# Lead-in of a two-layer kernel: image 0 convolved in whole chunks with a folded norm, stages without barriers

## The chip, the cores and the metric

The program runs on one core of one Trainium2 chip. The metric is the device time of one launch in microseconds, as the median of the runs. TensorE (PE) multiplies matrices and transposes, VectorE (DVE) and ScalarE (ACT) work element by element, GpSimd (POOL) computes powers and issues the gather, SyncE (SP) issues most DMAs. Each engine executes its instructions in order and waits on semaphores.

## What is computed

Four images of 384 channels and 56 x 56 pixels go through two layers, each with a residual. Cut to what matters here:

```python
# layer 0, on a group norm of x (32 groups)
value = dwconv3x3(x, w_v) ; query = dwconv3x3(x, w_q)
key   = dwconv3x3(x, w_k, stride=2) ; off = dwconv3x3(x, w_off1, stride=2)
o = gelu(layernorm_over_channels(off) * ln_g + ln_b)
pos = tanh(einsum(o, w_off2) + ref)            # 28 x 28 sampling points
v_sampled = bilinear_sample(value, pos)
attn = einsum('bcm,bcn->bmn', query, key) * SCALE
x = x + einsum(einsum(attn, v_sampled), w_out)
# layer 1, on a group norm of x
mid = silu(layernorm(xs) * ln_g + ln_b @ fc1_w + fc1_b) @ fc2_w + fc2_b
q, k, v = xs @ qkv_w ; q, k normed per head
o = norm(0.5 * v + q @ (k^T v) / pi) + mid
x = x + (o @ proj_w + proj_b)
```

Layer 0 is linear in the queries, so keys and sampled values are first multiplied into one small matrix per head, that is multiplied with `w_out` (W2T), and the "projection" is W2T times the queries.

## The kernel before

Channels are three chunks of 128 partitions; pixels are seven strips of 448 (8 rows), a strip four tiles of 112. Products that must be precise are made of three passes over a high and a low fp32r part (`WKVH`, `WKVL` and so on): `three_pass`. The program is written out by hand, engine by engine; the order in each engine's block is the order of execution, and every dependency is a semaphore.

A lead-in of four stages comes ahead of a loop over images. At the end of each stage every engine calls `stage_end` (line 292), which drains it and waits for all five.

- Stage 0 loads the weights into staging tiles (`stg`, `pst`, `qst`), folds layer norm's `ln_g` and a column centring into fc1, multiplies fc2 with proj into W2, splits the results into high and low parts, stores WKV to DRAM, and takes the group norm of image 0 from seven strips (`gn_coefs`, `gn_groups`). The small fc1-by-`ln_b` products stand first on TensorE (line 729), while the loads still run.
- Stage 1, `front(m, xg)` on each engine, seven times: ScalarE norms a strip into `XG`, VectorE does the value, key and offset taps (lines 1807, 448 or 112 columns) with the plain weights, TensorE the query taps as nine products with diagonal matrices (line 811) for each of three chunks, then transposes of values, keys and offsets; VectorE norms the offsets and takes their dot products. After the last strip come the sampling points.
- Stage 2: POOL gathers the value rows of 784 points from DRAM (`gather`, 14 indirect DMAs), VectorE mixes four neighbours (`sample_tile`), TensorE adds up key by value (`key_value`), then W2T.
- Stage 3, `project`: queries and residuals are loaded by strip, `project_strip` makes 27 passes, VectorE adds and takes the statistics of layer 1; meanwhile image 1 is read for its group norm and WKV is read back. Then `kv_start` norms the first strip, and the first key product of image 0 follows (line 892).

The image loop does layer 1 of image b, and beside it layer 0 of image b+1, which it already computes in another form than stage 1: the group norm is folded into the taps (`wfold`, `bfold`), image borders are filled with the group mean instead of zero so that the fold holds there, key and offset taps run over whole chunks of 784 outputs (line 2021), value and query taps over half chunks of 1568 (line 2233).

Of the kernel before, what the change touches and what calls it, by code (L numbers as in the profile page):

```python
# [12 lines left out]
P = 128  # L13
# [35 lines left out]
def constants():  # L49
# [6 lines left out]
    for k, (lo, hi) in enumerate(WIN):  # L56
# [6 lines left out]
    edge = np.ones((P, 2, STRIPS), f)  # L63
    edge[:, 0, 0] = 0
    edge[:, 1, STRIPS - 1] = 0
# [3 lines left out]
        "head0": head0, "head1": head1, "hsel": hsel, "refp": refp, "edge": edge,  # L69
# [3 lines left out]
def build(nc, d, out):  # L73
# [21 lines left out]
    with ctx:  # L95
# [13 lines left out]

        W1H, W1L = sb("W1H", [P, KC, HID], F32R), sb("W1L", [P, KC, HID], F32R)  # L110
        W2H, W2L = sb("W2H", [P, JC, C], F32R), sb("W2L", [P, JC, C], F32R)
        WQH, WQL = sb("WQH", [P, KC, C], F32R), sb("WQL", [P, KC, C], F32R)
        WPH, WPL = sb("WPH", [P, KC, C], F32R), sb("WPL", [P, KC, C], F32R)
# [3 lines left out]
        edge = sb("edge_s", [P, 2, STRIPS])  # L117
# [36 lines left out]
        WKVH, WKVL = sb("WKVH", [P, KC, 2 * C], F32R, at=at), sb("WKVL", [P, KC, 2 * C], F32R, at=at)  # L154
# [71 lines left out]
        at = [shared]  # L226
        pst = sb("pst", [P, KC, C], at=at)
        ones = sb("ones", [P, P], at=at)
        at = [shared + 14 * 1024]
        stg0, qst = sb("stg0", [P, KC * HID], at=at), sb("qst", [P, KC, 3 * C], at=at)  # L230
        assert at[0] <= wkv_at
        at = [base2]
        X0S = sb("X0S", [P, 3, KC, T], at=at)
        stg = [stg0, sb("stg1", [P, KC * HID], at=at)]


        at = [shared]
        diag = sb("diag", [P, KC, 9, P], at=at)
        XG2 = sb("XG2", [P, KC, RS + 2, W + 2], at=at)
        XR = sb("XR", [P, KC, RS + 2, W], at=at)  # L240
        XG = sb("XG", [P, KC, RS + 2, W + 2], at=at)
        VA, QA = sb("VA", [P, KC, T], at=at), sb("QA", [P, KC, T], at=at)
        VF = sb("VF", [TS, 2, C], at=at)
        KA, OA = sb("KA", [P, KC, TK], at=at), sb("OA", [P, KC, TK], at=at)
        KT, LN = sb("KT", [TK, C], at=at), sb("LN", [TK, C], at=at)
        olng, olnb = sb("olng", [TK, C], at=at), sb("olnb", [TK, C], at=at)
        woff2, prod = sb("woff2", [TK, 2, C], at=at), sb("prod", [TK, 2, C], at=at)
        obn, oag, orv = sb("obn", [TK, 6], at=at), sb("oag", [TK, 2], at=at), sb("orv", [TK, 2], at=at)
        dot = sb("dot", [TK, 2], at=at)
# [42 lines left out]
        def stage_end(eng, n):  # L292

            alone(eng)
            eng.drain().then_inc(stage_done, 1)
            eng.wait_ge(stage_done, n * 5 + 5)
            alone(eng)
# [2134 lines left out]
```

## Time and profile before

| | us |
|---|---|
| median of 3 runs (lowest, highest) | 3024.71 (3017.22, 3031.07) |
| profiled execution, its own time | 3018.12 |
| its span from first to last instruction | 3016.3 |
| TensorE busy | 2815.0 (93%) |
| VectorE busy | 2104.8 (70%) |
| ScalarE busy | 1201.0 (40%) |
| stages 0, 1, 2, 3 (length) | 99.4, 245.6, 44.0, 53.3 |

The stage ends are where the last engine leaves the barrier. Windows show each engine's busy time in a stretch and the clock granted to TensorE as a share of 2.4 GHz (0.50 is its lower level, 1.2 GHz). A group of the trace gives busy time, the mean length of one instruction and, behind the second bar, how long the engine stood idle before such instructions and for whom. TensorE's instructions overlap, so the distance from start to start is shorter than the length shown. An fp32 product is two instructions, one of fp32r a single one.

### The profile page before, as it was taken

What the parts mean: (1) busy time and instruction counts of PE and PEld (TensorE: products, weight loads), DVE (VectorE), ACT (ScalarE), POOL (GpSimd) and SP (SyncE); (2) the same over time, 40 slices, a digit from 0 to 9 for tenths busy, and PEclk for the clock granted to TensorE, in tenths of its full rate; (3) what the DMA queues carried; (4) which work ended last, traced back from release to release, by engine and by line L of the source; (5) the groups of instructions that cost most, each with busy time, mean ns of one, the idle gap of its engine ahead of it and who ended that gap; (6) DMA issues with size and microseconds to landing.
All of it is one profiled execution on the core that took longest, in us unless ns stands there. A gap on an engine that the chain in (4) does not pass through costs nothing.

```text
span 3016.3 us, 42244 instructions
## 1 busy us (share of the span) xinstructions
PE 2815.0 (93%) x14867; PEld 2535.9 (84%) x14867; DVE 2104.8 (70%) x3116; ACT 1201.0 (40%) x2089; POOL 690.4 (23%) x217
## 2 busy tenths in 40 slices
PE   5688578999999999999999999999999999999999
PEld 4344268989899889989999889989999899999998
DVE  3599768488888768488888768598788743444443
ACT  1433116634444226644433246544443244333332
POOL 0000104322222405222223215322223123311120
PEclk8888789999999999999999999999999999999999
DMA  5121583223322673222232763232333842111110
GB/s 203 49 79 64 159 305 124 90 66 108 108 95 93 204 257 118 84 91 91 92 123 84 248 208 114 70 111 92 102 101 114 269 173 84 34 50 37 44 40 28
DMA packets 187682, 347.54 MB, mean 115 GB/s; under 512 B 11040, under 2 KB 169312, under 8 KB 184912
## 3 DMA queue, kind: packets, MB, share of 16 engines
q1 hardware_dynamic: 180192, 320.72, 32.3%
q0 software_dynamic: 4480, 19.27, 2.2%
q10 hardware_dynamic: 2800, 4.82, 0.4%
q8 instruction: 124, 2.03, 0.3%
q14 instruction: 86, 0.70, 0.1%
HBM read 241.25 MB, written 103.51 MB: 114 GB/s over the span
## 4 chain that ended last, share of the span: by engine, by line
PE 68%; issue 12%; DVE 9%; DMA 6%; ACT 2%; POOL 1%; SPq 0%; DVEq 0%; ACTq 0%; POOLq 0%
PE bank L757 15%; PE bank L758 15%; PE bank L759 15%; PE bank L892 3%; PE bank L893 3%; PE bank L894 3%; PE bank L1092 3%; DVE VA L1807 3%; PE bank L914 3%; PE bank L1076 2%; DMA X<-x_scr 2%; DVE AC L2233 1%; DMA pair_scr<-VT 1%; PE bank L1043 1%; PE bank L1147 1%
## 5 line engine op out<-in xcount | busy, mean ns | idle before, releaser
L1567 ACT ACTIVATE S<-bank,b1p 128x448 f32<-128x448 f32 x336 | 212.9, 634 | 885.1 <-PE bank L759 864.7
L2233 DVE SCALAR_TENSOR_TENSOR AC<-XV,wfold,AC 128x1568 f32<-128x1568 f32 x288 | 530.4, 1847 | 3.1
L757 PE MATMUL bank<-SH,W2H 128*128 128x448 f32 x1008 | 394.9, 392 | 5.7 <-DVE SL L2202 5.6
L759 PE MATMUL bank<-SH,W2L 128*128 128x448 f32 x1008 | 379.6, 377 | 0.0
L758 PE MATMUL bank<-SL,W2H 128*128 128x448 f32 x1008 | 377.8, 375 | 0.0
L757 PE MATMUL bank<-XRH,W1H 128*128 128x448 f32 x1008 | 375.1, 372 | 0.0
L758 PE MATMUL bank<-XRL,W1H 128*128 128x448 f32 x1008 | 372.4, 369 | 0.0
L759 PE MATMUL bank<-XRH,W1L 128*128 128x448 f32 x1008 | 370.3, 367 | 0.0
L672 POOL TENSOR_TENSOR rq<-qn,nhalf 112x32 f32<-112x32 f32 x28 | 181.9, 6495 | 436.5 <-DVE qn L2172 436.5
L664 POOL TENSOR_TENSOR rk<-kn,nhalf 112x24 f32<-112x24 f32 (+1 forms) x56 | 200.8, 3598 | 294.5 <-DVE kn L1994 294.5
L2202 DVE TENSOR_TENSOR SL<-S,SH 128x448 fp32r<-128x448 f32 x336 | 208.0, 619 | 64.7 <-ACT SH L1570 64.6
L676 POOL TENSOR_TENSOR ro<-on,nhalf 112x32 f32<-112x32 f32 x28 | 179.8, 6422 | 311.3 <-DVE on L2193 311.2
L892 PE MATMUL bank<-WKVH,XH 128*112 128x384 f32 x672 | 234.4, 349 | 15.1 <-DVE XL L1961 7.4
L894 PE MATMUL bank<-WKVH,XL 128*112 128x384 f32 x672 | 227.8, 339 | 0.0
L893 PE MATMUL bank<-WKVL,XH 128*112 128x384 f32 x672 | 227.7, 339 | 0.0
L757 PEld LDWEIGHTS bank<-SH,W2H 128*128 128x128 f32 x1008 | 196.0, 194 | 21.8 <-issue 8.2
L759 PEld LDWEIGHTS bank<-SH,W2L 128*128 128x128 f32 x1008 | 195.8, 194 | 17.2
L758 PEld LDWEIGHTS bank<-SL,W2H 128*128 128x128 f32 x1008 | 196.5, 195 | 15.3 <-issue 0.3
L757 PEld LDWEIGHTS bank<-XRH,W1H 128*128 128x128 f32 x1008 | 193.0, 192 | 17.3
L759 PEld LDWEIGHTS bank<-XRH,W1L 128*128 128x128 f32 x1008 | 191.8, 190 | 16.7
L758 PEld LDWEIGHTS bank<-XRL,W1H 128*128 128x128 f32 x1008 | 192.0, 190 | 16.0
L1570 ACT ACTIVATE SH<-S 128x448 fp32r<-128x448 f32 x336 | 194.9, 580 | 16.3 <-ACT S L1567 0.8
(227 smaller groups left out, 5515.1 us busy)
## 6 DMA issues: line engine op xcount, KB each, us to landing
X<-x_scr SPq DMA_DIRECT2D x52, 672.0 KB, 5.3
XV<-in_xp SPq DMA_DIRECT2D x36, 870.0 KB, 6.6
CQ<-q_scr SPq DMA_DIRECT2D x28, 672.0 KB
CX<-in_x SPq DMA_DIRECT2D x28, 672.0 KB, 5.1
x_scr<-CX SPq DMA_DIRECT2D x28, 672.0 KB, 5.2
V<-v_scr SPq DMA_DIRECT2D x28, 672.0 KB, 4.7
Y<-x_scr SPq DMA_DIRECT2D x28, 672.0 KB
out<-Y SPq DMA_DIRECT2D x28, 672.0 KB, 3.8
```

The costliest lines, as they stand in the source:

```text
L664: pool.tensor_tensor(rk[:, lo:hi], kn[:, lo:hi], nhalf[0:TS, lo:hi], ALU.pow).then_inc(s["k_rs"], 1)
L672: pool.tensor_tensor(rq[:, :], qn[:, :], nhalf[0:TS, :], ALU.pow).then_inc(s["rq_s"], 1)
L757: mm(o, wh, xh, start=first, stop=False)
L758: mm(o, wh, xl, start=False, stop=False)
L759: return mm(o, wl, xh, start=False, stop=stop)
L892: mm(p, xh, WKVH[:, k, c0:c0 + C], start=(k == 0), stop=False)
L893: mm(p, xh, WKVL[:, k, c0:c0 + C], start=False, stop=False)
L894: last = mm(p, xl, WKVH[:, k, c0:c0 + C], start=False, stop=(k == KC - 1))
L1567: fn(S[:, j % 2, :], bank[j % 2][:, 0:T], ACT.Silu, bias=b1p[:, j:j + 1]).then_inc(s["s_s"], 1)
L1570: fn(SH[:, j % 3, :], S[:, j % 2, :], ACT.Copy).then_inc(s["sh"], 1)
L2202: tt(SL[:, j % 3, :], S[:, j % 2, :], f(SH[:, j % 3, :]), ALU.subtract).then_inc(s["sl"], 1)
L2233: stt(o, XV[h][:, ky:ky + HR, kx:kx + W], wfold[:, kind, k, 3 * ky + kx:3 * ky + kx + 1], o, ALU.mult, ALU.add).then_inc(s["va"], 1)
```

## The change

Image 0 is treated in the form that the image loop uses, and no stage has a barrier.

- The inputs come as three padded chunks (`XP`, 1.7 MB each) and the statistics are taken from them (`chunk_stats`); group norm is folded. Tables of the offset norm, the edge mask and `XR`, `XG` go.
- Weights are loaded into the place of their low parts (`fc1w` over `W1L`, `projw` over `WPL`, and so on) and split in place. TensorE begins with W2 (two banks instead of three), then group norm, then the fc1 and proj vector products. The splits of W1, WQ and WP and the centring of fc1 go between later work.
- Convolutions: key and offset taps on VectorE over whole chunks (`small_conv`, 48 taps); value taps of chunks 0 and 1 and query taps of chunk 2 on VectorE as six half chunks (`unit_conv`, 48 taps); value taps of chunk 2 and query taps of chunks 0 and 1 on TensorE (`front_taps`, 21 groups of nine products, with all other front work of TensorE and ScalarE placed between thirds of a group by `front_beside`).
- Offset norm, gelu and dot products are those of the image loop, on TensorE and ScalarE.
- The gather has four separate buffers; sample tiles 0 to 3 stand ahead of the last unit of query taps, 4 to 6 behind it. ScalarE issues the stores of TensorE's queries.

The diff, cut to its core:

```diff
-        def stage_end(eng, n):
-            alone(eng)
-            eng.drain().then_inc(stage_done, 1)
-            eng.wait_ge(stage_done, n * 5 + 5)
...
+            sp.dma_start(projw[:, :, :].rearrange("p k c -> p (k c)"), d["proj_w"]).then_inc(s["stg_ld1"], 16)
+            sp.dma_start(fc2w[:, :, :].rearrange("p k c -> p (k c)"), d["fc2_wT"]).then_inc(s["stg_ld1"], 16)
+            for k in range(KC):
+                sp.dma_start(XP[k][:, :, :], xpad_v[0, :, k, :, :]).then_inc(s[f"x0_ld{k}"], 16)
+            sp.dma_start(grp[:, :, :], d["grp"]).then_inc(s["grp_ld"], 16)
+            qkv_v = d["qkv_w"].rearrange("p (k c) -> p k c", k=KC)
+            sp.dma_start(kvw[:, :, :], qkv_v[:, :, C:3 * C]).then_inc(s["kvq_ld"], 16)
+            sp.dma_start(fc1w[:, :, :].rearrange("p k c -> p (k c)"), d["fc1_w"]).then_inc(s["stg_ld0"], 16)
...
+            sp.wait_ge(s["kt_st"], HEAD + 2 * KC * 16)
+            sp.wait_ge(s["gtp"], 2 * KC)
             load_sampling()
             load_output_weight()
-            for t in range(2):
-                load_queries(t)
-                load_residual(0, t)
-            stage_end(sp, 2)
+            for u in range(1, 4):
+                store_front_values(u)
+            for u in (4, 5):
+                sp.wait_ge(s[("q_st", "q_st1")[u % 2]], STRIPS * 16)
+                store_front_queries(u)
+            sp.wait_ge(s["q_st"], QST[0])
+            sp.wait_ge(s["q_st1"], QST[1])
+            load_queries(0)
+            load_queries(1)
+            sp.wait_ge(s["vs_s"], STRIPS)
+            load_residual(0, 0)
...
+            pool.wait_ge(s["dots"], HEAD + 1)
+            pool.wait_ge(s["kt_st"], HEAD + 2 * KC * 16)
+            pool.wait_ge(s["q0"], 2 * STRIPS)
+            for i in range(3):
+                pool.wait_ge(s[f"pair_st{i}"], VST[i])
+            gather(0, 0, STRIPS, GP)
...
+            def front_taps(m, j):
+                kind, k = front_part(m)
+                if j == 0:
+                    pe.wait_ge(s["diag_s"], m // STRIPS + 1)
+                    pe.wait_ge(s["bord"], 2 * KC)
+                    if m >= 3:
+                        pe.wait_ge(s["qa"], HEAD + m - 2)
...
+            for m in range(3 * STRIPS):
+                for j in range(3):
+                    front_taps(m, j)
+                    front_beside(3 * m + j)
...
+            act.wait_ge(s["gn_cf"], 2)
+            act.wait_ge(s["wkv_st"], 32)
+            front_centre(0)
+            front_diag(0)
+            front_centre(1)
+            front_diag(1)
...
+            gn_coefs(0, bank[4], bank[7], ((w2_lows(8, JC),), (wkv_low,), ()))
+            small_conv(0, 16)
+            dve.wait_ge(s["set_ps"], 1)
+            tt(b1p[:, :], b1[:, :], bank[0][:, 0:JC], ALU.add)
+            tt(bo[:, :], bp[:, :], bank[0][:, JC:JC + KC], ALU.add)
+            for k in range(KC):
+                last = ts_(fc1w[:, k, :], fc1w[:, k, :], lng[:, k:k + 1], None, ALU.mult)
+            last.then_inc(s["set_sum"], 1)
+            small_conv(16, 16)
+            centre_columns(0, 6, None)
+            centre_columns(1, 0, "set_sum")
+            small_conv(32, 16)
+            centre_columns(2, 6, "set_ctr")
+            unit_conv(0, 1, 8)
...
+            dve.wait_ge(s["w_h"], 2)
+            tt(WPL[:, :, :], projw[:, :, :], f(WPH[:, :, :]), ALU.subtract)
+            unit_conv(4, 1, 8)
+            for t in range(4):
+                sample_tile(0, t, GP, VSP)
+            unit_conv(5, 1, 8)
+            for t in range(4, STRIPS):
+                sample_tile(0, t, GP, VSP)
             key_value_heads(0)
-            key_value_low(0)
-            stage_end(dve, 2)
-
             project_low(0, 0)
             project_low(0, 1)
+            key_value_low(0)
+            dve.wait_ge(s["w_h"], 4)
+            tt(W1L[:, :, :], fc1w[:, :, :], f(W1H[:, :, :]), ALU.subtract)
+            tt(WQL[:, :, :], qw[:, :, :], f(WQH[:, :, :]), ALU.subtract)
```

How the instructions stand now. TensorE at the start of the program, first before (line 729 is fc1 by `ln_b`, 734 proj by `b2`, 791 the column means, 743 and 751 group norm, 801 W2; each count is of products):

```order
L729 MATMUL bank<-lnb,stg_170 128x1 x36
L734 MATMUL bank<-b_65,pst 128x1 x9
L791 MATMUL bank<-stg_170,ones 128x512 x9
L743 MATMUL bank<-gst,grp_s 128x4 x9
L751 MATMUL bank<-gdev,grp_s 128x4 x9
L801 MATMUL bank<-pst,stg_173 128x384 x36
```

and now, up to the first pieces of the front:

```order
L724 MATMUL bank<-projw,fc2w 128x384 x36
L734 MATMUL bank<-gst,grp_s 128x4 x9
L742 MATMUL bank<-gdev,grp_s 128x4 x9
L759 MATMUL bank<-lnb,fc1w 128x1 x36
L763 MATMUL bank<-b_68,projw 128x1 x9
L787 MATMUL bank<-XC_172,diag 128x448 x15
L838 MATMUL bank<-ident_s,QA_180 112x128 x4
L787 MATMUL bank<-XC_172,diag 128x448 x3
L802 MATMUL bank<-ident_s,KA_112 112x128 x4
L787 MATMUL bank<-XC_172,diag 128x448 x3
```

W2 moved from last to first, the vector products from first to behind group norm, and the column means into the taps. TensorE in a strip of the front before (taps at 811, transposes at 766, 785 and 773):

```order
L811 MATMUL bank<-XG,diag 128x448 x9
...
L766 MATMUL bank<-ident_s,OA 112x128 x3
L811 MATMUL bank<-XG,diag 128x448 x18
...
L785 MATMUL bank<-ident_s,VA 112x128 x9
...
L773 MATMUL bank<-ident_s,KA 112x128 x3
```

and now from tap group 9 on (851 transposes value unit 0, 820 the normed offsets back):

```order
L787 MATMUL bank<-XC_121,diag 128x448 x6
L851 MATMUL bank<-ident_s,AP_173 112x128 x10
L787 MATMUL bank<-XC_121,diag 128x448 x3
L851 MATMUL bank<-ident_s,AP_173 112x128 x4
L787 MATMUL bank<-XC_121,diag 128x448 x3
L820 MATMUL bank<-ident_s,OTP 128x112 x4
L787 MATMUL bank<-XC_121,diag 128x448 x3
L820 MATMUL bank<-ident_s,OTP 128x112 x4
```

Transposes stand between thirds of a tap group instead of behind a strip. VectorE from the last sample tile to the first residual add, before:

```order
L1923 SCALAR_TENSOR_TENSOR VS<-G_160,W_93,VS 112x384 x3
L1929 TENSOR_TENSOR MT<-bank,head_s 128x384
L1936 TENSOR_TENSOR W2TL<-bank,W2TH 128x384 x3
L1942 TENSOR_TENSOR CL<-CQ_135,CH 128x1344
L1942 TENSOR_TENSOR CL<-CQ_137,CH 128x1344
L1949 TENSOR_TENSOR CX_130<-CX_130,bank 128x448 x3
```

and now, from sample tile 3 on:

```order
L1933 SCALAR_TENSOR_TENSOR VSP<-GP_189,W_96,VSP 112x384 x3
L2020 SCALAR_TENSOR_TENSOR AP_174<-XC_172,wfold,AP_174 128x1568 x8
...
L1939 TENSOR_TENSOR MT<-bank,head_s 128x384
L1952 TENSOR_TENSOR CL<-CQ_139,CH 128x1344
L1952 TENSOR_TENSOR CL<-CQ_141,CH 128x1344
L1946 TENSOR_TENSOR W2TL<-bank,W2TH 128x384 x3
L2089 TENSOR_TENSOR W1L<-fc1w,W1H 128x4608
L2090 TENSOR_TENSOR WQL<-qw,WQH 128x1152
L1959 TENSOR_TENSOR CX_134<-CX_134,bank 128x448 x3
```

The last unit of query taps stands between the sample tiles, and the two weight splits ahead of the first residual add.

## Rows read from the trace of the kernel before

**Rows 1.** The page's part 1 (busy us by engine) and granted clock, 40 slices.

```profile
PE 2815.0 (93%) x14867; PEld 2535.9 (84%) x14867; DVE 2104.8 (70%) x3116; ACT 1201.0 (40%) x2089; POOL 690.4 (23%) x217
...
PEclk8888789999999999999999999999999999999999
```

**Rows 2.** Windows by stage: us, busy PE, PEld, DVE, ACT, POOL, clock, DMA, GB/s.

```profile
0.00:99.40 99.40, 64.42 (x216) 46.21 (x216) 40.16 (x74) 15.57 (x17) 1.78 (x7) 0.90 0.41 154
99.40:345.00 245.60, 180.81 (x504) 92.77 (x504) 216.45 (x616) 91.94 (x181) 6.41 (x7) 0.84 0.22 72
345.00:389.00 44.00, 15.57 (x48) 11.33 (x48) 18.29 (x34) 1.48 (x3) 13.72 (x14) 0.52 0.75 215
389.00:442.30 53.30, 43.07 (x189) 38.23 (x189) 41.74 (x66) 9.21 (x7) 0.00 (x0) 0.90 0.96 342
442.30:1085.00 642.70, 617.90 (x3440) 577.68 (x3440) 504.05 (x632) 283.79 (x493) 179.57 (x51) 0.97 0.38 124
```

**Rows 3.** Timeline, PE, 458 to 463 us: the first key product of image 0.

```profile
462.73 0.66 PE L892 MATMUL bank<-WKVH,XH 128*112 128x384 f32 x1 [7.44 <-DVE XL L1961]
```

**Rows 4.** By line, PE, 0 to 445 us: busy us, mean | idle.

```profile
L811 PE MATMUL bank<-XG,diag 128*128 128x448 f32 x378 | 162.4, 591 | 25.9 <-ACT diag L1374 18.8 <-DVE XG L1791 7.1
L801 PE MATMUL bank<-pst,stg 128*128 128x384 f32 x72 | 26.3, 529 | 0.2 <-DVE W2L L1784 0.2
...
L729 PE MATMUL bank<-lnb,stg 128*128 128x1 f32 x72 | 15.5, 352 | 17.7 <-DMA pst<-in_proj_w 17.7
L785 PE MATMUL bank<-ident_s,VA 128*112 128x128 f32 x84 | 11.9, 278 | 16.5 <-ACT VF L1348 14.4 <-DVE LN L1834 2.1
```

**Rows 5.** Timeline, PE, 135 to 160 us: start, length, line, count.

```profile
134.50 5.42 PE L811 MATMUL bank<-XG,diag 128*128 128x448 f32 x14
140.67 1.17 PE L785 MATMUL bank<-ident_s,VA 128*112 128x128 f32 x9 [0.74 <-DVE LN L1834]
...
149.67 9.84 PE L811 MATMUL bank<-XG,diag 128*128 128x448 f32 x18 [1.05 <-DVE XG L1791]
```

**Rows 6.** Timeline, DVE, 496 to 499 us: small taps in the first image.

```profile
497.02 1.04 DVE L2021 SCALAR_TENSOR_TENSOR OA<-XC,wfold,OA 128x784 f32<-128x784 f32 x1
497.96 1.04 DVE L2021 SCALAR_TENSOR_TENSOR KA<-XC,wfold,KA 128x784 f32<-128x784 f32 x1
```

**Rows 7.** Groups by line, DVE, 442 to 1085 us: large taps in the images.

```profile
L2233 DVE SCALAR_TENSOR_TENSOR AC<-XV,wfold,AC 128x1568 f32<-128x1568 f32 x96 | 176.8, 1847 | 1.0
```

**Rows 8.** Groups by line and shape, DVE, 0 to 445 us.

```profile
L1714 DVE BATCH_NORM_STATS2 bst<-X0S 128x6 f32<-128x448 f32 x42 | 23.2, 614 | 20.8 <-DMA X0S<-in_x 20.7
...
L1781 DVE TENSOR_TENSOR W1L<-stg,W1H 128x4608 fp32r<-128x4608 f32 x1 | 5.0, 4955 | 0.0
```

**Rows 9.** DMA issues, 0 to 100 us: KB each, us from issue to landing.

```profile
wkv_scr<-WKVL SPq DMA_DIRECT2D x1, 1152.0 KB, 6.5
```

**Rows 10.** Windows of 1 us around the second strip's start.

```profile
145.00:146.00 1.00, 0.00 (x0) 0.00 (x0) 1.00 (x5) 0.00 (x0) 0.00 (x0) 0.56 0.93 353
155.00:156.00 1.00, 1.00 (x4) 0.56 (x3) 1.00 (x5) 0.00 (x0) 0.00 (x0) 0.81 0.08 31
```

**Rows 11.** Timeline, POOL and DVE, 345 to 360 us: gather and first tile.

```profile
346.56 1.14 POOL L639 DMA_INDIRECT G<-pair_scr,IX  x1 [19.76 <-issue]
...
357.64 0.42 DVE L1920 TENSOR_SCALAR VS<-G,W 112x384 f32<-112x384 f32 x1 [12.52 <-DMA G<-pair_scr,IX]
358.09 1.93 DVE L1923 SCALAR_TENSOR_TENSOR VS<-G,W,VS 112x384 f32<-112x384 f32 x3
```

**Rows 12.** Timeline, DVE and PE, 390 to 402 us: start of the projection.

```profile
391.21 3.03 DVE L1942 TENSOR_TENSOR CL<-CQ,CH 128x1344 fp32r<-128x1344 f32 x2 [2.37 <-ACT CH L1395]
...
400.89 0.62 DVE L1949 TENSOR_TENSOR CX<-CX,bank 128x448 f32<-128x448 f32 x1 [1.24 <-PE bank L759]
...
392.87 0.71 PE L757 MATMUL bank<-CH,W2TH 128*128 128x448 f32 x1 [5.15 <-DVE CL L1942]
```

**Rows 13.** The gather's line, whole run: ns min/median/max of one.

```profile
L639 POOL DMA_INDIRECT G<-pair_scr,IX x56: 931/966/3160, 346.6 to 2362.4; - x56
```

More of the change, by code:

```diff
@@ new lines, in front_bank7, with turn_front_keys @@
+            def front_bank7(keys, offsets):
+                pe.wait_ge(s["kt_ev"], HEAD + keys)
+                pe.wait_ge(s["ln1"], offsets)
+            def turn_front_keys(k, g):
+                pe.wait_ge(s["ka"], HEAD + k * 8 + 8)
+                front_bank7(2 * k + g, STRIPS if k == 2 else 0)
+                for i in range(GT[g]):
+                    t = g * GT[0] + i
+                    last = tr(bank[7][0:TK, i * P:(i + 1) * P], KA2[:, k % 2, t * TK:(t + 1) * TK], ident[:, :])
+                last.then_inc(s["ktp"], 1)
@@ new lines, in front_dots, with turn_strip @@
+            def front_dots():
+                pe.wait_ge(s["gelu"], KC)
+                for t in range(STRIPS):
+                    for k in range(KC):
+                        last = mm(bank[7][0:TK, 2 * t:2 * t + 2], GEP[:, k, t * TK:(t + 1) * TK], woff2c[:, k, :],
+                                  start=(k == 0), stop=(k == KC - 1))
+                last.then_inc(s["dots"], 1)
+            def turn_strip(m):
+                pe.wait_ge(s["qa"], HEAD + m + 1)
+                if m >= 2:
+                    pe.wait_ge(s["vt_ev"], HEAD + m - 1)
+                for j in range(SUB):
+                    last = tr(bank[4 + m % 2][0:TS, j * P:(j + 1) * P], QA[m % 2][:, j * TS:(j + 1) * TS], ident[:, :])
+                last.then_inc(s["vtp"], 1)
@@ new lines, in unit_conv @@
+            def unit_conv(u, first, count):
+                kind, k, h = front_unit(u)
+                for i in range(first, first + count):
+                    if i == 1:
+                        dve.wait_ge(s["v0"], 2 * u + 2)
+                    else:
+                        dve.wait_ge(s["va"], HEAD + u * 8 + i - 1)
+                    ky, kx = TAPS[i]
+                    o = AP[h][:, :].rearrange("p (r w) -> p r w", w=W)
+                    stt(o, XP[k][:, ky + h * HR:ky + h * HR + HR, kx:kx + W], wfold[:, kind, k, 3 * ky + kx:3 * ky + kx + 1], o,
+                        ALU.mult, ALU.add).then_inc(s["va"], 1)
@@ new lines, in centre_columns @@
+            def centre_columns(q, p, sg):
+                dve.wait_ge(s["set_ps"], q + 2)
+                for k in range(KC):
+                    v = fc1w[:, k, q * 512:(q + 1) * 512]
+                    last = tt(v, v, bank[p][:, :], ALU.subtract)
+                if sg is not None:
+                    last.then_inc(s[sg], 1)
+            for j in range(4):
+                w2_low(j)
+            chunk_stats(0)
+            w2_low(4)
+            w2_low(5)
+            chunk_stats(1)
+            w2_low(6)
@@ new lines, in _ @@
+            last.then_inc(s["set_sum"], 1)
[5 more added lines that the diff above has]
+            unit_conv(0, 1, 8)
+            for t in range(STRIPS):
+                dve.wait_ge(s["ln1"], t + 1)
+                dve.bn_stats(obn7[:, t, :], OTP[:, t, :]).then_inc(s["obn_s"], 1)
+            dve.wait_ge(s["obn_s"], STRIPS)
+            for t in range(STRIPS):
+                last = dve.bn_aggr(oag7[:, t, :], obn7[:, t, :])
```

776 lines of the change are left out of this document (385 added, 391 removed).

## The prediction, made blind

> **What bounds the kernel now.** I first read the busy shares and the clock line of the page [rows 1]: TensorE is busy 93% of the span, but its first slices (75 us each) read 5, 6, 8, 8 tenths and then nothing but 9. So the images after the lead-in are full, and what can be won lies ahead of them. Then the windows of the four stages [rows 2]: 99.4 us of weight preparation, 245.6 us of convolutions on image 0, 44 us of sampling, 53.3 us of projection; the first key product of image 0 starts at 462.7 us [rows 3]. Stage 1 is held by VectorE (216.5 of 245.6 us busy), stage 2 by the gather (VectorE 18.3 and TensorE 15.6 of 44 us busy, DMA share 0.75), stage 3 by transfers (share 0.96). The first image's 643 us hold 618 us of TensorE. The change touches none of the images' instructions, so I take 462.7 us to the end as fixed: the whole question is where the first key product starts afterwards.
>
> **Who bounds the new lead-in.** The same 189 fp32 tap products of 448 columns stay on TensorE; each is two instructions (378 rows at L811 [rows 4]), and in a stretch at the full clock one starts every 0.38 us (14 in 5.42 us, [rows 5]). That is 143.6 us (162.4 busy before, low clock included). VectorE loses the small taps: before, a strip of an image needed 24+24+24 taps, 504 in all; afterwards it has 48 taps of 784 columns, one every 0.95 us (start to start in [rows 6]), and 48 of 1568 columns at 1.85 us [rows 7], so 45.6 + 88.7 = 134 us, and with statistics, splits and seven sample tiles about 170 us. TensorE has 143.6 us of taps plus 31 us of other work between them (below), 175 us, and it starts later. Both are near each other, but the code makes VectorE wait for TensorE (its sample tile 2 needs the first key-value product, which stands behind all 21 tap groups), so I follow TensorE.
>
> **Step A, up to the first tap product.**
> (1) TensorE now begins with the W2 products. They need the constants, proj_w and fc2: as many bytes as fc1 and proj before, whose end let L729 start at 17.7 us [rows 4]. 17.7.
> (2) The W2 products: 72 instructions took 26.3 us of TensorE [rows 4], low clock at their start included. New is that three chunk statistics of seven bn_stats stand between their low parts on VectorE; one lasts about 0.55 us net (23.2 us for 42, [rows 8]), so 3.9 us a chunk. With two banks, each pause costs what exceeds the product in hand (about 1.9 us): three times 1 to 2.4 us, 5 us. To 49 us.
> (3) Group norm: twice 18 instructions on 4 columns, weight-bound like those of (4): 4 us each at 0.215 an instruction, half of it while the clock is high as it is after (2), and 1 us of VectorE between: 54 us (58 at most).
> (4) The fc1-by-ln_b and proj-by-b2 products, 90 instructions of one column. Before, they ran while the first loads came in; now nothing covers them. L729 shows 15.5 us for 72, 0.215 each [rows 4]: 19.4 us, to 73.5. Should they run at the high clock it is half. ScalarE is not later: WKVL is split by 54.5 us, its store lands 6.5 us after issue [rows 9], and centre taps and the first nine diagonals take 5 us more, 66.5.
>
> **Step B, the 21 tap groups.** 143.6 us, plus: 84 value transposes, 63 of keys, offsets and back, at 0.13 us each (11.9 us for 84 is an upper sum [rows 4]; nine took 1.17 us [rows 5]), 19 us; 42 instructions of the offset dots at the same 0.11, 4.6 us; 18 of the column means, 512 columns, 0.38 x 512/448 = 0.43, 7.7 us. Together 31.4 us. The start is at the low clock: of 149.67 to 155.6 us, 0.75 us an instruction [rows 5, 10], which loses 3 us. One wait is on the path: the transposes back of the offsets stand behind group 10; they need the normed tiles, and these need VectorE's unit 0 (14.8 us, begun only when the third column mean is subtracted), seven tile statistics, three taps of unit 1, the shift and four ScalarE rows. I get 5 us of idle TensorE there, and the clock falls after such a gap: it read 0.56 in the microsecond from 145 on, after a few short transposes and two gaps of 2 to 3 us, and came back only within 155 to 156, 6 us into the next taps [rows 10]; 3 us more. Sum: 143.6 + 31.4 + 3 + 5.3 + 3 = 186 us, so the last tap ends at 260 us. Other handovers have slack: values out of unit 0 are ready about 2 us before TensorE asks, all others 8 us and more. VectorE idles some 28 us on column means and dots, which costs nothing. SP waits for the offsets' way back (about 188 us) before it loads the key tile, with the value stores of unit 1 queued behind; TensorE turns these only at 190 us, so nobody waits. ScalarE now issues the 14 query stores, one per tap group of 7 us, with two buffers; a store of that size lands within 3 us.
>
> **Step C, the tail.** Key-value product 0 (0.7), sample tiles 2 and 3 at 2.4 us (0.42 + 1.93, [rows 11]), then unit 5 of the query taps, 14.8 us: 280.3. Two chains leave from there. Queries: store and reload, 4.5 and 5 us, to 290, then ScalarE's copy and two splits of 1.5 us [rows 12]. Samples 4 to 6, 7.2 us, to 287.5, head product and W2T, 5.9 us as before, but VectorE's splits lie between: the first projection product at 295.7. Two weight splits that stood in stage 0, W1L (5 us, [rows 8]) and WQL (a quarter of its columns, 1.4 us), now stand on VectorE ahead of the first residual add and hold it to 302, while the products of this strip (8 us at a rising clock, [rows 12]) end at 304; its last add is done at 304.6, before at 401.5 [rows 12]. That is 96.9 us sooner. The gather isn't on the path: its stores are done at 235 us, the first tile came 11 us after the first issue [rows 11], 246, and the path asks for tiles 2 and 3 at 261.
>
> **Step D, projection.** Bound by transfers before, of the same bytes now. The 19 us ahead of the first add must carry both queries, three residual strips, three strips for statistics and 1.4 MB of weights, 6.9 MB at the 342 GB/s of [rows 2], 20 us; before, part of it had landed in stage 2. I take the rest, 401.5 to 462.7, as unchanged, so the first key product at 366 us.
>
> **Barriers.** Their removal by itself is nearly nothing in the sum: between the stages only 1 to 3 us pass. What counts is that stores, gather and weight splits then lie beside taps.
>
> **Sum.** 3018.1 us of the profiled execution less 96.9 is 2921. The profiled run was 6.6 us under the median of the three runs shown (3024.7), so for a median I say 2928.
>
> **The gather under the taps.** Of 56 issues in the whole run the median took 0.97 us, the longest 3.16 [rows 13]; those of stage 2 ran beside an almost idle VectorE, those of the images beside a busy one. I take the median and keep 3.16 as the bound: eight issues (tiles 0 to 3) from 235 us at 3.16 + 0.3 end at 262.7 instead of 245, and their data comes 8.7 us later (11.1 less the first two issues), so tile 3 would be ready at 271 and not by 263.
> By the Trainium skill, "SBUF — State Buffer", section "SBUF: two separate sides", VectorE and GpSimd share one port pair that one instruction locks for its whole length, and POOL's descriptor writing starves behind it; moving the gather from an idle VectorE under its taps goes against that page. By its lock each of the eight issues would wait for up to a tap, by the row's median none does; that is rival R3, and the sum above goes by the median.
>
> **Rivals.**
> (R1) Many handovers instead of one. TensorE's order now has some 45 foreign pieces between taps, each with its own wait; before it had three a strip and the clock of the stage was 0.84 [rows 2]. If it is 0.84 here too, 175 us at full clock take 208, 22 us more than my 186 has for clock and wait net of 11; with a few us of waits, 2945 to 2965. For it: 144.9 us. Against: 14 instructions without a gap in 134.5 to 140.
> (R2) One-column products at the high clock and no gap at the offsets: 10 and 8 us less, 2905 to 2915. Against: L729 kept 0.215 us for 15 us on end.
> (R3) The gather's issues all take the longest time seen: tile 3, and with it unit 5 and all behind it, is 8 us late: 2936, inside my range. For it: nothing covers POOL but luck in the order; against: the median is that of the idle case.
> (R4) Slower: the mixed stream of fp32 taps and 112-column transposes never brings the clock up. Then 175 us take 350, 164 more than my sum has net of its 11: 3018 - 97 + 164 = 3085 profiled, 3092. It turns slower once the mean granted clock of the front is below 0.62 (175 / 283). Against: 1.00 in the same taps before.
> (R5) It doesn't overlap: ScalarE, with stores to issue and six kinds of rows, holds each group by 4 us: 21 x 4 = 84 us, 3012. Against: its rows sum to some 75 us, three banks cover it.
>
> **How the numbers follow.** Forecast 0.62 (2915 to 2945), R1 0.20, R2 0.08, R3 0.03, R5 0.03, R4 0.04. The range 2905 to 2960 takes in R2, R3 and most of R1 and leaves out a part of R1, R4, R5 and what may lie below. About 0.5% (15 us) is what a measurement of this kernel can tell from no change; faster by more 0.93 (forecast, R1, R2, R3), within it 0.03 (R5), slower 0.04 (R4).
>
> **What would show it.** The first tap product at 70 to 78 us (A), the last at 250 to 270 us (B), an idle of TensorE of about 5 us after group 10, a granted clock over 0.9 between; VectorE's first residual add at 301 to 305 us (C); the first key product at 360 to 372 us (D); images of the same 643 us. It is wrong if TensorE waits in the front for more than 15 us in all, or if the images change.

## The result, and the profile of the changed kernel

The changed kernel took 2891.6 us (median of four runs, 2886.4 to 2895.5) against 3025.8 us of the kernel before (four runs, 3017.2 to 3031.1, those of the prediction among them): a ratio of 0.9574, with a 95% interval of 0.9551 to 0.9597. It is 134 us faster. The prediction said 97 us and 2928 us, with a range down to 2905: the sign was right, the time was outside the range, 36 us lower. The profiled execution took 2895.5 us with a span of 2893.7.

I read the new trace in the order of the prediction's steps. First the windows by stage, which answer to [rows 2]: up to the first tap product, the taps, the tail to the first projection product, the projection; columns as there.

```profile
core 0: us, PE busy (x) PEld busy (x) DVE busy (x) ACT busy (x) POOL busy (x), PEclk, DMA share, GB/s
0.00:72.50 72.50, 50.70 (x199) 38.13 (x199) 32.88 (x67) 22.89 (x49) 1.78 (x7) 0.85 0.55 216
72.50:257.20 184.70, 179.13 (x588) 97.52 (x589) 131.92 (x136) 62.86 (x99) 15.92 (x13) 0.95 0.29 82
257.20:292.30 35.10, 13.05 (x49) 9.15 (x47) 30.93 (x35) 4.64 (x6) 3.75 (x2) 0.56 0.50 170
292.30:345.20 52.90, 43.73 (x189) 38.80 (x189) 44.29 (x65) 6.64 (x5) 0.00 (x0) 0.90 0.94 329
```

In the taps' stage TensorE is busy for 179 of 184.7 us, which makes it the one that bounds the stage (the runs on the lead-in below test that). In the 35 us of tail VectorE is busy for 30.9, and the projection has a DMA share of 0.94, as before. Now TensorE's timeline at the places that the prediction named (start, duration, count, and in brackets the idle time and its releaser).

```profile
start us, us, engine line op out<-in xcount [idle before <-releaser]
16.49 3.91 PE L724 MATMUL bank<-projw,fc2w 128*128 128x384 f32 x7 [16.49 <-DMA fc2w<-in_fc_wT]
...
53.37 15.40 PE L759 MATMUL bank<-lnb,fc1w 128*128 128x1 f32 x72
68.64 3.98 PE L763 MATMUL bank<-b,projw 128*128 128x1 f32 x18
...
167.21 0.98 PE L820 MATMUL bank<-ident_s,OTP 112*128 112x112 f32 x4 [5.20 <-ACT OTP L1419]
...
364.96 0.66 PE L946 MATMUL bank<-WKVH,XH 128*112 128x384 f32 x1 [6.25 <-DVE XL L1971]
```

and VectorE's tail, cut to what the end of the lead-in hangs on:

```profile
start us, us, engine line op out<-in xcount [idle before <-releaser]
258.01 0.42 DVE L1930 TENSOR_SCALAR VSP<-GP,W 112x384 f32<-112x384 f32 x1 [11.79 <-PE bank L895]
...
262.60 15.06 DVE L2020 SCALAR_TENSOR_TENSOR AP<-XC,wfold,AP 128x1568 f32<-128x1568 f32 x8
...
292.19 4.95 DVE L2089 TENSOR_TENSOR W1L<-fc1w,W1H 128x4608 fp32r<-128x4608 f32 x1
297.06 1.35 DVE L2090 TENSOR_TENSOR WQL<-qw,WQH 128x1152 fp32r<-128x1152 f32 x1
298.32 1.15 DVE L1959 TENSOR_TENSOR CX<-CX,bank 128x448 f32<-128x448 f32 x2
```

| step of the prediction | forecast, us | in the trace, us |
|---|---|---|
| W2 products begin | 17.7 | 16.5 |
| one-column products begin, end | 54, 73.5 | 53.4, 72.5 |
| idle after group 10 | 5.3 | 5.2 |
| last tap product ends | 260 | 257.2 |
| first residual add starts | 302 | 298.3 |
| first key product starts | 366 | 365.0 |
| image 0, key product to the next group norm | 643 (unchanged) | 642.9 (before 644.5) |
| first key product to the end | 2555 (unchanged) | 2528.7 (before 2553.6) |

So the lead-in as a whole came out as forecast, 97.8 us shorter where 96.9 was said. What was missing lies behind it, in the part that I took as fixed. The windows of the four images, before and after, from the first key product or from the group norm of the next image to the next one; first those of before:

```profile
462.70:1107.20 644.50, 630.45 (x3513) 588.80 (x3514) 510.72 (x634) 283.75 (x493) 178.20 (x50) 0.98 0.39 126
1107.20:1768.50 661.30, 647.27 (x3586) 603.22 (x3585) 516.48 (x651) 289.82 (x502) 179.37 (x51) 0.97 0.40 128
1768.50:2430.40 661.90, 645.44 (x3585) 602.01 (x3584) 516.40 (x651) 289.95 (x502) 179.36 (x51) 0.98 0.39 128
2430.40:3016.30 585.90, 579.95 (x3195) 545.49 (x3193) 237.29 (x366) 215.46 (x379) 130.19 (x36) 0.98 0.17 53
```

and of after:

```profile
365.00:1007.90 642.90, 628.86 (x3513) 591.39 (x3514) 510.19 (x634) 282.94 (x493) 177.46 (x50) 0.97 0.40 127
1007.90:1661.50 653.60, 642.31 (x3587) 604.96 (x3585) 516.01 (x651) 289.16 (x502) 178.81 (x51) 0.97 0.40 129
1661.50:2314.40 652.90, 640.78 (x3585) 602.92 (x3584) 516.20 (x651) 289.04 (x502) 178.81 (x51) 0.97 0.41 129
2314.40:2893.70 579.30, 573.26 (x3195) 544.88 (x3194) 237.27 (x366) 215.04 (x379) 130.16 (x36) 0.98 0.17 54
```

The counts agree within two records, VectorE and ScalarE do the same in the same time, and yet images 1 to 3 are 7.7, 9.0 and 6.6 us shorter. TensorE's own time fell (5.0, 4.7 and 6.7 us). Over a whole tile of the last image nothing has gone away: the same products stand in both traces, and the changed kernel gains about 0.09 us every 4 to 5 us. That points to the time of each single product. I followed the same 133 intervals between products of 448 columns without a gap, at the full clock. Of before, the second row and the last but one are the ends:

```profile
2620.33 0.46 PE L757 MATMUL bank<-SH,W2H 128*128 128x448 f32 x1
2620.63 0.36 PE L758 MATMUL bank<-SL,W2H 128*128 128x448 f32 x1
...
2647.76 0.36 PE L759 MATMUL bank<-XRH,W1L 128*128 128x448 f32 x1
2647.96 0.27 PE L1043 MATMUL bank<-ident_s,X 128*112 128x128 f32 x1
```

and of after:

```profile
2501.86 0.46 PE L748 MATMUL bank<-SH,W2H 128*128 128x448 f32 x1
2502.16 0.37 PE L749 MATMUL bank<-SL,W2H 128*128 128x448 f32 x1
...
2528.77 0.36 PE L750 MATMUL bank<-XRH,W1L 128*128 128x448 f32 x1
2528.97 0.27 PE L1097 MATMUL bank<-ident_s,X 128*112 128x128 f32 x1
```

The 133 intervals took 27.13 us before and 26.61 after: 204.0 and 200.1 ns from start to start. The durations of the rows (0.36, 0.37) do not show it, only the starts do. Over all images the mean is 203.5 ns before and 200.2 after, and some 7,500 of their products have 448 columns, run at the full clock and follow one another without a gap: 7,500 x 3.3 ns is 25 us.

### The profile page after: what moved, and what is told of

The parts are those of the page before. It is cut to its first block, busy times and chain, and to the rows that moved or that the text cites. A ratio compares the mean times of both kernels' runs of the same rounds, so it can differ in the third digit from the quotient of the medians.

```text
span 2893.7 us, 41252 instructions
## 1 busy us (share of the span) xinstructions
PE 2779.8 (96%) x14930; PEld 2535.6 (88%) x14930; DVE 2027.5 (70%) x2630; ACT 1177.1 (41%) x2040; POOL 688.1 (24%) x211
## 4 chain that ended last, share of the span: by engine, by line
PE 79%; issue 8%; DMA 6%; DVE 5%; ACT 2%; SPq 1%; POOL 0%; ACTq 0%; DVEq 0%; POOLq 0%
PE bank L748 16%; PE bank L750 16%; PE bank L749 16%; PE bank L787 4%; PE bank L946 4%; PE bank L948 3%; PE bank L947 3%; PE bank L1146 3%; PE bank L968 3%; PE bank L1130 2%; DMA X<-x_scr 2%; PE bank L1097 1%; PE bank L1201 1%; DMA pair_scr<-VT 1%; DMA X0Q<-in_x 1%
## 5 line engine op out<-in xcount | busy, mean ns | idle before, releaser
L748 PEld LDWEIGHTS bank<-SH,W2H 128*128 128x128 f32 x1008 | 196.0, 194 | 16.5 <-issue 5.2
```

The costliest lines, as they stand in the source:

```text
L748: mm(o, wh, xh, start=first, stop=False)
```

## Theory and experiments on the images

In one place the kernel before has 200 ns as well: the products of the projection, `CH` by `W2TH`, 200.1 to 200.2 ns. That speaks against the chip or its clock. What the change did to the images without a word is this: it dropped the tile `edge_s`, 56 bytes per partition that take up 64, out of the middle of the SBUF list, and so all tiles of the images behind it lie 64 bytes lower. The addresses per partition in bytes, taken modulo 128, of the weights (W1, W2, WQ, WP) and of what is streamed past them (XR, S, M, X): before 0 and 0, after 0 and 64.

Theory A (A1 and A2 below are its two readings): TensorE streams the pixels of one product and loads the weights of the next at the same time, and where both start at the same place modulo 128 bytes each product is 4 ns longer. Rival B: the traces differ by chip, code or place in DRAM.

The shift alone, in the kernel before (`before_shift`):

```diff
-        edge = sb("edge_s", [P, 2, STRIPS])
...
         kv_end = at[0]
+        edge = sb("edge_s", [P, 2, STRIPS], at=at)
```

> The kernel before with one change: the 64-byte tile edge_s is allocated behind all others and no longer in the middle, so every tile behind it lies 64 bytes lower in SBUF, as it does in the changed kernel; no instruction is added or taken away. Theory A (the images became faster because the pixels that TensorE streams no longer start on the same multiple of 128 bytes as the weights): products of 448 columns start every 200 ns instead of 204, about 7,500 of them, so the images lose 25 us and the median falls from 3026 to about 3001; the lead-in stays at 462.7 us. Rival B (the traces differ by chip, placement in memory or code, not by address in SBUF): 204 ns and 3026 us as before.

Measured: 2996.8 us against 3017.4 of the kernel before beside it, a ratio of 0.9916 (0.9892 to 0.9941): 21 us by the medians, 25 by the ratio. The first key product stood at 465.2, 2.5 us later than before, so all of the gain is in the images (2533.0 us instead of 2553.6 in the profiled executions). The same 133 intervals took 26.61 us, 200.1 ns each:

```profile
2606.66 0.37 PE L758 MATMUL bank<-SL,W2H 128*128 128x448 f32 x1
...
2633.27 0.36 PE L759 MATMUL bank<-XRH,W1L 128*128 128x448 f32 x1
```

The reverse, in the changed kernel (`after_shift`):

```diff
         hsel = sb("hsel_s", [P, KC, NH1])
+        pad64 = sb("pad64", [P, 16])
```

> The changed kernel with 64 bytes of padding where edge_s was, so that all tiles behind it lie at the addresses modulo 128 that they had before. Theory A: products back at 204 ns in the images, 2892 + 25 = 2917 us, first key product still at 365 us. Rival B: 200 ns and 2892 us.

Measured: 2910.5 us, a ratio of 0.9641 (0.9618 to 0.9665), 0.7% or 20 us above the changed kernel's ratio; first key product at 366.4. In the profiled executions the images took 2538.8 us instead of 2528.7, 10 us more and not the 25 that theory A gave; where the rest went is worked out below. The 133 intervals took 27.13 us again:

```profile
2506.48 0.36 PE L750 MATMUL bank<-SL,W2H 128*128 128x448 f32 x1
...
2533.61 0.36 PE L751 MATMUL bank<-XRH,W1L 128*128 128x448 f32 x1
```

So rival B falls in both directions: the time of a product goes with the address. Next, whether it is the streamed tile's own address or its distance from the weights (`after_both`, and the mirror of the changed kernel, `w64_s0`):

```diff
+        pad_w = sb("pad_w", [P, 16])
         fc2w, fc1w = sb("fc2w", [P, KC, HID], at=list(top)), sb("fc1w", [P, KC, HID], at=[top[0] + KC * HID * 4])
...
-        b1p, b1 = sb("b1p", [P, JC]), sb("b1", [P, JC])
+        b1p = sb("b1p", [P, JC])
...
         kv_end = at[0]
+        b1 = sb("b1", [P, JC], at=at)
```

(`w64_s0` has the first line alone.)

> The changed kernel with the weights W1, W2, WQ, WP moved up by 64 bytes (one small bias tile goes to the end to make room), the streamed tiles unmoved: weights and pixels are then both at 64 modulo 128. Theory A1 (it matters that the two are equal modulo 128): 204 ns, 2917 us. Theory A2 (it matters that the streamed tile starts on a multiple of 128): 200 ns, 2892 us.

> The changed kernel with every tile 64 bytes higher: weights W1, W2, WQ, WP at 64 modulo 128, streamed tiles XR, S, M, X at 0. The mirror of the changed kernel (weights 0, streamed 64: 200 ns); equal positions took 204 ns at 0 and 0, and 203 to 205 at 64 and 64. Theory A1 (what matters is the distance of 64 between the two): 200 ns, as the changed kernel, 0.957 of the kernel before. Theory A2 (a streamed tile at 0 costs, whatever the weights): 204 ns, 0.964. Theory A3 (both must lie where the changed kernel has them): 202 to 205 ns, mixed.

And one look with four places in one kernel (`after_classes`):

```diff
+        PHASE = {"XRH": 0, "SH": 32, "MH": 96, "WKVH": 0}
...
+            while name in PHASE and at[0] % 128 != PHASE[name]:
+                at[0] += 32
```

> The changed kernel with each streamed tile at another address modulo 128, weights at 0: inputs of fc1 (XRH, XRL) at 0, of fc2 (SH, SL) at 32, of proj (MH, ML) at 96, of the query product (XH, XL) at 64; and the key-value weights WKVH, WKVL, which are streamed there, at 0 beside XH at 64, where both were at 64. Theory A1 or A2: only the fc1 products are at 204 ns (2,800 of them, so about 10 us), the other classes at 200. Should 32 and 96 cost too, a start modulo 64 counts. The key-value products stood at 176 ns with both tiles alike in either kernel; if equality costs them as well they fall by about 3 ns, if their weight load bounds them they stay.

Measured: `after_both` 2900.6 us, 0.9605 (0.9576 to 0.9634); `w64_s0` 2890.5 us, 0.9573 (0.9548 to 0.9598), the changed kernel's own ratio; `after_classes` 2908.7 us in its one run. The interval of `after_both` overlaps the changed kernel's (0.9551 to 0.9597), and its 2900.6 us are far from the 2917 of theory A1, so its time alone decides nothing between A1 and A2; the intervals do. The stretch of 133 comes six times in its last image and took 26.95 to 27.49 us; in `w64_s0` it took 26.61 us each time. The ends of one such stretch, first in `after_both`, then in `w64_s0`:

```profile
2565.07 0.36 PE L751 MATMUL bank<-SL,W2H 128*128 128x448 f32 x1
...
2592.03 0.36 PE L752 MATMUL bank<-XRH,W1L 128*128 128x448 f32 x1
```

and:

```profile
2489.28 0.37 PE L750 MATMUL bank<-SL,W2H 128*128 128x448 f32 x1
...
2515.88 0.36 PE L751 MATMUL bank<-XRH,W1L 128*128 128x448 f32 x1
```

The mean start-to-start time in the images, from all products of 448 columns with no gap and at the full clock (from some 700 in one class of one kernel to 7,500):

| weights, streamed (mod 128) | seen in | ns |
|---|---|---|
| 0, 0 | before, after_shift; XR in after_classes | 202 to 205 |
| 64, 64 | after_both | 202 to 206 |
| 0, 64 | before_shift, changed kernel; X in after_classes | 198 to 202, mean 200.2 |
| 64, 0 | w64_s0 | 198 to 202, mean 200.2 |
| 0, 32 | S in after_classes | 201.5 to 201.9 |
| 0, 96 | M in after_classes | 204.9 to 205.4 |

So the distance counts, not the place: 64 bytes apart is fast from either side, and equal is slow at either. That is theory A1. The runs show that the time hangs on the distance; that weight load and stream meet in the memory, as theory A supposes, they do not show. The bytes between are less clean: 96 was as slow as equal, 32 in between, and the projection's products, 32 apart in every kernel but `after_classes`, had means of 200 to 201 ns in five kernels and 202 to 204 in seven. What else sets those is open. The key-value products (384 columns, weights of 112 columns) kept 174 to 179 ns in every kernel, at a distance of 0 or of 64; their weights begin 448 bytes apart, so that both distances come by turns within each kernel.

By the Trainium skill, "TensorE: Matmul & The Clock Gate", section "Step-by-step: what each phase is for", TensorE has two independent read ports, and loading the next weights does not steal read bandwidth from the running product. At the size of 4 ns in 204 the traces here don't fit that well: the time of a product hangs on where its stream lies relative to the weights.

That the images changed by 25 us in all is a balance of several things. I split TensorE's time in the images into four parts: what products of 448 and 384 columns take beyond 200 and 176 ns each, as long as the next product starts within 230 ns (the spacing); what they take beyond that when the next one starts later, idle time left out (the long steps; more than half of it falls where the granted clock reads 0.50); idle time; and all other products.

| us | spacing | long steps | idle | others |
|---|---|---|---|---|
| before | 23.4 | 80.8 | 44.9 | 415.4 |
| before_shift | -0.7 | 88.2 | 41.3 | 415.0 |
| changed kernel | -1.6 | 85.1 | 37.8 | 418.2 |
| after_shift | 23.7 | 73.2 | 37.9 | 415.0 |
| after_both | 23.8 | 75.9 | 31.9 | 414.2 |
| w64_s0 | -0.9 | 75.9 | 40.3 | 412.8 |

The spacing makes 24 to 25 us in both pairs. The rest moves as well: from before to the changed kernel the long steps took back 4 us, other products 3, and idle time gave 7; in `after_shift` the long steps gave back 12 and the others 3 of the 25 us that the spacing cost, which leaves the 10 us. Image 0 kept only 1.6 of its 6 us, since 3 went to long steps and 1 to others. The shift raised the time of the long steps in both pairs, by 7 and 12 us. Whether denser products cause that these runs don't settle: over all kernels here the images took 2516.4 to 2533.0 us with the two tiles 64 bytes apart and 2534.9 to 2553.6 with them alike (`after_classes`, which is mixed, left out). Each group spreads over 17 to 19 us, and their means lie 19 us apart.

## Experiments on the lead-in

The forecast of the lead-in hit to within a microsecond, and a sum can do so by luck. Five runs test its terms.

Step A, the one-column products on the path (`no_columns`), with only the first of three parts of each column of `b1p` and `bo` left:

```diff
-                for k in range(KC):
+                for k in range(1):
                     mm(bank[0][:, j:j + 1], fc1w[:, k, j * P:(j + 1) * P], lnb[:, k:k + 1],
-                       start=(k == 0), stop=(k == KC - 1))
+                       start=(k == 0), stop=(k == 0))
```

(and the same for `projw` by `b2`; the kernel leaves out 75 of the 90 instructions)

> The changed kernel, leaving out 75 of the 90 one-column products (of every column of the folded bias only one of its parts is computed, so its biases are incomplete). Theory A (they stand on the path, from 53.4 to 72.3 us, with ScalarE's first nine diagonal blocks next, ready at 66.8): first tap product at 66.8 instead of 72.5, and everything behind it 5.7 us earlier: last tap 251.5, first key product 359.3, the whole 5.7 us shorter than the changed kernel. Rival B (VectorE's chain to the offsets or the gather sets the end of the lead-in): first tap earlier, first key product still at 365. Rival C: without them TensorE pauses for 7 us before the taps, the clock is low for longer, and less than 3 us are left of the gain.

```profile
65.93 2.61 PE L787 MATMUL bank<-XC,diag 128*128 128x448 f32 x3 [7.53 <-ACT diag L1385]
...
356.40 0.66 PE L946 MATMUL bank<-WKVH,XH 128*112 128x384 f32 x1 [6.25 <-DVE XL L1971]
```

The first tap is 6.6 us earlier and waits for ScalarE's diagonals, as said; the last tap ends at 250.3, 6.9 us earlier, the first key product is at 356.4, 8.6 earlier, 1.6 of them in the projection. Theory A had said 359.3. The ratio, 0.9562 (0.9530 to 0.9593), agrees but its interval holds no gain as well; the trace decides, for theory A.

Step B, the wait for the offsets (`early_mean`):

```diff
-                elif i == 21:
+                elif i == 15:
                     pe.wait_ge(s["set_sum"], 2)
                     column_means(2, 6)
...
                         front_unit_out((28, 36, 42, 48).index(i), g)
+                    if i == 28:
+                        front_norms()
...
-                    if u == 0:
-                        front_norms()
...
-            unit_conv(1, 1, 3)
+            unit_conv(1, 1, 1)
             dve.wait_ge(s["orr_s"], 1)
...
-            unit_conv(1, 4, 5)
+            unit_conv(1, 2, 7)
```

> The changed kernel with the third column mean taken 6 pieces earlier (after the taps of piece 15 and not of 21), so that VectorE begins unit 0 some 14 us earlier, and with ScalarE's seven normed rows right behind the values of unit 0. Theory A (the 5.2 us of idle TensorE after group 10 come from VectorE's late unit 0, as the prediction says, and cost 3 us of low clock behind them): no idle there, last tap at 249 to 252 instead of 257, first key product at 357 to 360. Rival B (VectorE sets the end of the lead-in, since sample tiles and unit 5 come behind one another on it): the last tap is earlier and the first key product moves by 0 to 2 us.

```profile
160.95 0.55 PE L820 MATMUL bank<-ident_s,OTP 112*128 112x112 f32 x4
161.34 2.43 PE L787 MATMUL bank<-XC,diag 128*128 128x448 f32 x6
165.19 0.57 PE L820 MATMUL bank<-ident_s,OTP 112*128 112x112 f32 x4 [1.42 <-ACT GEP L1425]
```

The wait of 5.2 us is gone; 1.4 us for the next copy are left. The low clock is gone too: behind the old gap the six taps took 4.71 us, now 2.43. From first to last tap it is 178.1 us and no longer 184.7, 6.6 less: 3.8 of idle, and 2.8 that I put down to the clock (the six taps account for 2.3 of it, the four transposes ahead of them for 0.4), where the prediction had put 3. The clock row of the changed kernel at that place:

```profile
167.20:172.50 5.30, 5.29 (x11) 2.73 (x12) 5.19 (x4) 2.08 (x4) 0.00 (x0) 0.50 0.00 0
172.50:180.00 7.50, 7.50 (x29) 4.41 (x28) 7.39 (x5) 2.17 (x4) 0.00 (x0) 0.97 0.08 31
```

After 5.2 us of idle it stood at 0.50, the 1.2 GHz level, for the first 5.3 us of work. The first key product is at 354.6, 10.4 us earlier and better than the 357 to 360 of theory A: 6.6 us in the taps, 2.9 in the projection, and 0.9 ahead of the first tap, which this edit doesn't touch. The ratio is 0.9537 (0.9502 to 0.9572). Rival B falls.

Step C, the tail (`unit5_first`), and the two moves together (`both_moves`):

```diff
-            for t in range(4):
+            for t in range(2):
                 sample_tile(0, t, GP, VSP)
             unit_conv(5, 1, 8)
-            for t in range(4, STRIPS):
+            for t in range(2, STRIPS):
                 sample_tile(0, t, GP, VSP)
```

> The changed kernel with VectorE's unit 5 of the query taps ahead of sample tiles 2 and 3 and no longer behind them. Theory A (the tail is VectorE's: 11.8 us in which it waits for key-value product 0 and so for the last tap are filled by unit 5): tile 2 at 261 us, the last sample tile done at 274 instead of 284.4, first key product at 354 to 356. Rival B (the gather takes the place: its last tile is asked for only when tile 2 has been read, at 263, under idle VectorE, and its data comes 8 to 11 us later): last sample tile at 274 to 277, first key product 356 to 359. Rival C (the projection is bound by transfers that start no earlier): first key product at 363 or later.

```profile
244.52 15.06 DVE L2020 SCALAR_TENSOR_TENSOR AP<-XC,wfold,AP 128x1568 f32<-128x1568 f32 x8
...
272.24 0.42 DVE L1930 TENSOR_SCALAR VSP<-GP,W 112x384 f32<-112x384 f32 x1 [3.49 <-DMA GP<-pair_scr,IX]
```

Unit 5 now fills the wait, and the first key product is at 355.4, 9.6 us earlier, 1.2 of them ahead of the first tap, which the edit doesn't touch. The wait for the last gathered tile takes 3.5 us of the gain, which is rival B's mechanism; the end that B forecast (356 to 359) was too late. The ratio is 0.9535 (0.9498 to 0.9573). So the tail was VectorE's, as the prediction had it.

> The two moves together. If each is on a path of its own, first key product at 347 to 352, and 14 to 18 us less than the changed kernel, a ratio to the kernel before of about 0.952; if they share one wait (both shorten the time to key-value product 0), no better than the one move of unit 5: 355 us and 0.954.

Measured: first key product at 348.0, 2867.8 us, a ratio of 0.9511 (0.9474 to 0.9548). By the traces the two moves together give 17.0 us of the 20.0 that they give one by one, so most of each is on a path of its own. By its median this is the fastest kernel of the study.

The splits W1L and WQL, 6.3 us ahead of the first residual add, looked like the next thing to move (`late_w1`, on top of `both_moves`):

```diff
-            dve.wait_ge(s["w_h"], 4)
-            tt(W1L[:, :, :], fc1w[:, :, :], f(W1H[:, :, :]), ALU.subtract)
-            tt(WQL[:, :, :], qw[:, :, :], f(WQH[:, :, :]), ALU.subtract)
...
                 strip_stats(1, t)
+                if t == 3:
+                    dve.wait_ge(s["w_h"], 4)
+                    tt(W1L[:, :, :], fc1w[:, :, :], f(W1H[:, :, :]), ALU.subtract)
+                    tt(WQL[:, :, :], qw[:, :, :], f(WQH[:, :, :]), ALU.subtract)
```

> The two moves of the kernel both_moves, and in addition the two weight splits W1L and WQL (6.3 us of VectorE) moved from ahead of the first residual add to behind the statistics of strip 3, where VectorE waits for TensorE. Theory A (they hold the first residual add, not transfers): the first residual add starts 3 to 5 us earlier, at 279 to 281 instead of 283.6, and the first key product 1 to 4 us earlier than the 348.0 of both_moves. Rival B (the projection is bound by its transfers, which start with the last sample tile): first add earlier, first key product at 348 or later, by up to 3 us since strip 4 now stands behind the splits.

```profile
279.65 0.62 DVE L1959 TENSOR_TENSOR CX<-CX,bank 128x448 f32<-128x448 f32 x1 [2.26 <-PE bank L750]
...
283.19 0.62 DVE L1959 TENSOR_TENSOR CX<-CX,bank 128x448 f32<-128x448 f32 x1 [1.18 <-PE bank L750]
...
312.43 4.94 DVE L2093 TENSOR_TENSOR W1L<-fc1w,W1H 128x4608 fp32r<-128x4608 f32 x1
```

The first add starts 4.2 us earlier, and the first key product 5.6 us later, at 353.6 (0.9532, 0.9495 to 0.9569, an interval that overlaps that of `both_moves`). At the start little was to be had: each of the strip's adds now waits for TensorE, and the last one ends 1.7 us earlier and not 4.2. In the middle of the projection the splits hold the low part of strip 5 and with it TensorE, which waits 6.7 us. I had expected at most 3 us of loss.

## Why the prediction was right and where it was wrong

- **The sum for the lead-in** held, in part by luck: 97.8 us against 96.9. Steps A, B and C each came out 1 to 2 us shorter than forecast, and D longer: from the end of strip 0's last add (300.3) to the first key product were 64.7 us, not the 61.2 taken over from before. Errors of -1.0, -1.8, -1.5 and +3.5 us nearly cancel. Why the projection took longer stays open: from the first add's start to the key product the kernels with the same order there lie between 63.8 and 67.5 us.
- **Who bounds the lead-in** held: TensorE through the taps (`no_columns` and `early_mean` move the last tap by what they take from it), then VectorE (`unit5_first`).
- **The clock**: 0.95 in the taps, so R1 (many handovers) and R4 (never high) did not happen. R2's first half fell as well: the 90 one-column products took 19.1 us, 0.21 each, at a granted clock of 0.50. That the higher level would halve them, as the prediction says, fits their neighbours: 18 group norm products of 4 columns took 2.07 us at 1.00 just before and 3.97 us at 0.50 behind the projection. R2's argument against itself, 0.215 for 15 us on end, was therefore a product time at the lower level. The row for stage 0 in [rows 2] doesn't show that: before its first recorded change, at 46.1 us, the clock of such a window counts as 1.00. R2's time, 2905 to 2915, would have been nearer to the result, by a mechanism that was not there; its other half, no gap, is what `early_mean` makes.
- **The gather**: its 14 issues had a median of 0.93 us and the path did not wait as R3 has it. But those that ran beside taps took longer, 2.12 and 1.39 us at 232 to 236 and 2.77 at 262.5; unit 4's taps had ended at 235.1, and most issues found VectorE idle. In `unit5_first` two more fell under taps, 1.76 and 1.58 us. The first of them, the fastest kind, and the last:

```profile
232.08 2.12 POOL L631 DMA_INDIRECT GP<-pair_scr,IX  x1 [70.06 <-issue]
...
237.43 0.93 POOL L631 DMA_INDIRECT GP<-pair_scr,IX  x1 [0.30 <-issue]
...
262.49 2.77 POOL L631 DMA_INDIRECT GP<-pair_scr,IX  x1 [0.30 <-issue]
```

  The Trainium skill, "SBUF — State Buffer", section "SBUF: two separate sides", has conditions that the prediction leaves out: for a VectorE instruction with two SBUF inputs, as the taps are, it gives the lock only against a GpSimd instruction that reads SBUF, and it tells of starved descriptors for VectorE's two-port modes. The rows above agree with a lock in kind; which of the two cases this is, no run here shows. The median served because the order left most issues a VectorE without taps, and not because issues beside taps take the median.
- **The step that failed** is the sentence that took 462.7 us to the end as fixed, because the change touches none of the images' instructions. It does not touch them, but it moves all their tiles from `wconv` on by 64 bytes, and the full diff has the dropped tile. The images came out 24.9 us shorter, which is 25 of the 36 us missed. The shift by itself accounts for 21 us by the medians in the kernel before and for 20 by the ratios in the changed one; the 4 or 5 us left are not pinned to a cause.
- **The median**: 6.6 us were added since the profiled execution of before lay that much under its median. The profiled execution of after lay 3.9 us above its own, so the two make 10.5 us; the 0.9 left are the lead-in.
- **R1's rows**: the "144.9 us" that R1 gives for itself stands in none of the rows shown; what they have near it is the clock of 0.56 in the microsecond from 145 on [rows 10].

The range was built from the costs in the lead-in alone. It left out any mechanism behind the first key product, on 85% of the span.

## What to carry to other kernels

When a diff drops or adds a tile in a bump allocator, list the new addresses of everything behind it before calling the rest of the kernel fixed; 64 bytes were worth 0.7 to 0.8% here. Compare two traces by the start-to-start time of the same long gapless stretch, since durations of single rows hide such a difference. And where an engine waits for a buffer at the end of a stage, look for work that only stands behind the wait by order: moving unit 5 gave some 9 us for two changed numbers.

## What the hardware showed that was not expected

- Products of 448 fp32r columns with weights of 128 columns: 200.1 ns start to start where weights and streamed tile are 64 bytes apart modulo 128, 204.0 where they are equal (0 and 0). Eight kernels with the first distance and two with the second showed it in the stretch of 133 without exception; with both at 64 the same stretch varied between 202.6 and 206.7 ns a product.
- Issuing one gather from GpSimd took 0.93 us beside an idle VectorE and 1.4 to 2.8 us where it began under taps that start every 1.85 us.
- The granted clock was 0.50 behind 5.2 us of idle TensorE and cost 2.8 us, less than the idle itself.
